# Causal mask of the key-major scores: a VectorE addition in place of a TensorE product

## What is computed

```
q = (x @ Wq) as 32 heads;  k, v = halves of x @ Wkv       # one key/value head
scores = q k^T / sqrt(32) + slope[h] * (kpos - qpos)
scores = where(kpos <= qpos, scores, -inf)                # the causal mask
attn = softmax(scores) @ v;  x = layernorm(x + attn @ Wo)
x = layernorm(x + x @ W^T + b + lora_of_selected_rank(x))
```

## Time and profile before

| what | value |
|---|---|
| median of three runs | 3512.88 us (3511.38 to 3514.06) |
| the profiled execution | 3511.45 us, span of its records 3509.7 us |
| attention proper (first to last S) | 55.6 to 2647.7 us of the span |
| mean granted TensorE clock | 0.978 of full speed |

### The profile page before, as it was taken

One profiled execution on the slowest core, in us unless ns is written; L12 is line 12 of the kernel. 1 busy time (PEld: TensorE's weight loads), 2 busy tenths in 40 slices (PEclk: granted clock), 3 DMA queues, 4 the chain that ended last, 5 costly groups with the idle time before them and its releaser, 6 DMA issues. The chain is left out here.

```text
span 3509.7 us, 55953 instructions
## 1 busy us (share of the span) xinstructions
PE 3387.2 (97%) x20577; PEld 2208.8 (63%) x20577; DVE 2120.3 (60%) x5166; ACT 1715.1 (49%) x3076; POOL 1593.7 (45%) x484
## 2 busy tenths in 40 slices
PE   6989999999999999999999999999997999999998
PEld 4655555555655554555555555555535999999997
DVE  4556667776877662566676677876723545454544
ACT  2536647667656666546566666666673101010100
POOL 1114536666577775125356656676892101010100
PEclk8999999999999999999999999999997999999999
DMA  3531221111110112332131211111102121212121
GB/s 103 146 91 56 73 71 52 49 49 53 42 52 25 49 32 81 111 88 79 52 88 43 58 28 52 43 28 40 58 31 85 55 72 54 72 54 72 54 72 43
DMA packets 214076, 215.45 MB, mean 61 GB/s; under 512 B 13876, under 2 KB 162356, under 8 KB 213784
## 3 DMA queue, kind: packets, MB, share of 16 engines
q1 hardware_dynamic: 213848, 212.46, 20.6%
HBM read 144.72 MB, written 67.17 MB: 60 GB/s over the span
## 5 line engine op out<-in xcount | busy, mean ns | idle before, releaser
L1041 ACT ACTIVATE prob<-ps_s,alibi 128x512 f32<-128x512 f32 (+3 forms) x2049 | 1220.1, 630 | 698.8 <-PE ps_s L1314 658.7
L976 POOL TENSOR_TENSOR prob<-prob 128x2048 f32<-128x2048 f32 (+1 forms) x240 | 1043.7, 4367 | 314.8 <-PE ps_o L1321 235.7
L1158 DVE TENSOR_REDUCE mxp<-ps_a 128x1 f32<-128x512 f32 x1536 | 972.8, 682 | 345.2 <-PE ps_a L1297 339.0
L1297 PE MATMUL ps_a<-wol,qst 97*128 97x512 f32 (+3 forms) x2560 | 934.9, 383 | 36.3 <-DVE mxp L1158 11.4
L1314 PE MATMUL ps_s<-qst,kexp 97*128 97x512 f32 (+3 forms) x2049 | 832.9, 411 | 5.5 <-ACT prob L1041 4.7
L1161 DVE CUSTOM_DVE_ANT_0 ps_a<-ps_a,maska 128x128 f32<-128x128 f32 (+3 forms) x1024 | 484.9, 513 | 305.4 <-PE ps_a L1297 282.6
L1263 PE MATMUL ps_m<-woh,wol 128*128 128x512 f32 x1704 | 646.6, 412 | 4.5 <-POOL wol L961 4.4
L1297 PEld LDWEIGHTS ps_a<-wol,qst 97*128 97x128 f32 x2560 | 486.7, 192 | 200.3 <-DVE mxp L1158 68.8
L1321 PE MATMUL ps_o<-prob,val 128*32 128x512 f32 (+3 forms) x5120 | 565.1, 537 | 11.4 <-ACT prob L1041 8.7
L1314 PEld LDWEIGHTS ps_s<-qst,kexp 97*128 97x128 f32 x2049 | 400.6, 196 | 193.4 <-ACT prob L1041 117.7
L961 POOL TENSOR_TENSOR wol<-wq_raw,wol 128x1024 fp32r<-128x1024 f32 x64 | 152.4, 2381 | 653.1 <-ACT wol L1016 653.1
(11 more groups left out here) (133 smaller groups left out, 3415.9 us busy)
## 6 DMA issues: line engine op xcount, KB each, us to landing
qst<-q_rows SPq DMA_DIRECT2D x192, 256.0 KB, 3.9
work<-in_L_attn_hidden_states SPq DMA_DIRECT2D x64, 512.0 KB, 4.9
wq_raw<-in_L_attn_Wq SPq DMA_DIRECT2D x64, 512.0 KB, 4.8
q_rows<-wol SPq DMA_DIRECT2D x128, 256.0 KB, 2.0
att_scratch<-at_sb SPq DMA_DIRECT2D x64, 256.0 KB, 2.5
at_raw<-att_scratch SPq DMA_DIRECT2D x32, 512.0 KB, 5.3
out<-work SPq DMA_DIRECT2D x32, 512.0 KB, 3.1
work<-in_L_attn_Wo SPq DMA_DIRECT2D x8, 512.0 KB, 4.4
```

What stands on the lines that cost most here:

```text
L976: nc.gpsimd.tensor_tensor(even[:, :, c1:], even[:, :, c1:], odd[:, :, c1:], ALU.add).then_inc(pair_done, 1)
L1041: nc.scalar.activation(prob[slot_of(step)][:, h, c0:], bank[:, c0:], ACT.Exp, bias=alibi_of(g, h, k - full_tiles(g))).then_inc(e_done, 1)
L1158: nc.vector.tensor_reduce(top, ps, AX.X, ALU.max).then_inc(a_done, 1)
L1297: last = nc.tensor.matmul(bank[:, 0:cols], qst[g % 3][0:KR, h, t * P:(t + 1) * P], kmax[0:KR, ring(sg):ring(sg) + cols], start=True, stop= ...
```

## The change

The mask products and `identb` go. `maskt` becomes f32, and VectorE adds it to the 128 diagonal columns of the score bank in place, between the score matmul and the exponential. The exponential of a diagonal tile waits for a new counter, `masked`, where it waited for `s_full`. The planner books 270 ns on VectorE (its next item 190 ns after) in place of 41 ns on TensorE, and so writes a different order.

```diff
+def masks_until(g, k, h):
+    return GH * (QT * g + k - full_tiles(g)) + h + 1
...
         if k >= full_tiles(g):
-            self.pe, end = self.pe + 41, end + 41
+            end = self.on_dve(end + 37, 270, 190) - 4
...
-        identb = sb(ctx, "identb", [P, P], BF16)
-        maskt = sb(ctx, "maskt", [P, P], BF16)
+        maskt = sb(ctx, "maskt", [P, P], F32)
...
-                act.wait_ge(s_full, START + scored + 1)
+                if k >= full_tiles(g):
+                    act.wait_ge(masked, START + masks_until(g, k, h))
+                else:
+                    act.wait_ge(s_full, START + scored + 1)
...
+            def mask(g, k, h, bank, scored):
+                c0 = (k - full_tiles(g)) * P
+                tile = bank[:, c0:c0 + P]
+                dve.wait_ge(s_full, START + scored + 1)
+                nc.vector.tensor_tensor(tile, tile, maskt[:], ALU.add).then_inc(masked, 1)
...
                 if what == "A":
                     maximum(n, *arg, banks[bank], at)
+                if what == "S" and arg[0] >= full_tiles(n):
+                    mask(n, *arg, banks[bank], at)
...
-                if diagonal:
-                    nc.tensor.matmul(bank[:, c0:c0 + P], identb[:], maskt[:], start=True, stop=False,
-                                     skip_group_check=True)
                 last = nc.tensor.matmul(bank[:, c0:], kexp[0:KR, at:at + P], qst[g % 3][0:KR, h, c0:],
-                                        start=not diagonal, stop=True, skip_group_check=True)
+                                        start=True, stop=True)
```

More of the change, by code:

```diff
@@ L815, in attention @@
         s_full = counter("s_full")
+        masked = counter("masked")
         e_done = counter("e_done")
@@ L939, in _ @@
             nc.gpsimd.memset(ident[:], 0.0).then_inc(pool_c, 1)
-            nc.gpsimd.memset(identb[:], 0.0).then_inc(pool_c, 1)
             nc.gpsimd.memset(maska[:], 0.0).then_inc(pool_c, 1)
@@ L944, in _ @@
             nc.gpsimd.iota(dist_i[:], [[P, DIST0 + QT]], base=-P * DIST0, channel_multiplier=1).then_inc(pool_c, 1)
+            pool.wait_ge(pool_c, 5)
+            nc.gpsimd.iota(kpos_i[3 * DH:KR], [[1, QB]], base=0, channel_multiplier=0).then_inc(pool_c, 1)
             pool.wait_ge(pool_c, 6)
[L946 to L950, removed]
+            nc.gpsimd.affine_select(out=ident[:], in_=ident[:], compare_op=ALU.not_equal, fill=1.0, base=0,
+                                    pattern=[[-1, P]], channel_multiplier=1).then_inc(pool_c, 1)
             nc.gpsimd.affine_select(out=maska[:, QB - P:], in_=maska[:, QB - P:], compare_op=ALU.is_ge, fill=MASKED, base=0,
@@ L954, in _ @@
                                     pattern=[[1, P]], channel_multiplier=-1).then_inc(pool_c, 1)
-            pool.wait_ge(pool_c, 11)
+            pool.wait_ge(pool_c, 9)
             nc.gpsimd.memset(kexp[3 * DH:KR].bitcast(F32), 1.0).then_inc(ones_row, 1)
@@ L1102, in distances @@
             def distances():
-                dve.wait_ge(pool_c, 7)
+                dve.wait_ge(pool_c, 6)
                 nc.vector.tensor_copy(dist[:], dist_i[:]).then_inc(dist_done, 1)
@@ L1227, in _ @@
         def _(pe):
-            pe.wait_ge(pool_c, 11)
+            pe.wait_ge(pool_c, 9)
             pe.wait_ge(slope_set, NH)
@@ L1308, in scores @@
                 c0 = max(0, k - full_tiles(g)) * P
-                diagonal = k >= full_tiles(g)
                 at = key_tile(g, k) * P
-                if diagonal:
-                    nc.tensor.matmul(bank[:, c0:c0 + P], identb[:], maskt[:], start=True, stop=False,
-                                     skip_group_check=True)
                 last = nc.tensor.matmul(bank[:, c0:], kexp[0:KR, at:at + P], qst[g % 3][0:KR, h, c0:],
-                                        start=not diagonal, stop=True, skip_group_check=True)
+                                        start=True, stop=True)
                 last.then_inc(s_full, 1)
```

## The result

The changed kernel took 3585.84 us as the median of four runs (3569.97 to 3591.40), the kernel before 3512.26 (3511.38 to 3514.06): a ratio of 1.0201, 95% interval 1.0166 to 1.0237. It is 74 us slower, where 43 us faster was forecast, and lies outside the range.

The account below looks back on a forecast made before the run. TensorE was taken to set the pace over most of the attention. Terms -123 + 20 + 30 + 19 + 11 = -43 us took the profiled 3511.45, plus 1.4 for the median, to 3470 us; range 3398 to 3530.

Parts of the forecast that it names:

- What the change removes: TensorE, diagonal tiles: dropping 1,024 mask products at 0.12 us each saves 123 us, if TensorE sets the pace at each.
- What it adds: VectorE: 1,024 additions of 128x128 at 0.24 us each in the queue (ends 0.127 and 0.315), 246 us in all.
- What waits behind it: Runs of diagonal tiles: TensorE waits for VectorE from the fourth tile on, costing 20 + 30 + 19 us.
- What moves: Planner's new order: 53 more returns from P or U to wide products at 0.21 us each, 11 us.
- Rival 2: Diagonal tiles: VectorE becomes the bound, every pair with an A at 0.85 us; 3639, in part slower by less; chance 0.18.
- Rival 1: Attention: no new waits, since the planner's P, U and Q cover VectorE everywhere; 3401 us; chance 0.19.
- Rival 3: Attention stages: another engine ends them, so waits fill the product's removal; 3513 us, give or take 10; chance 0.13.

## Why the prediction was wrong

Its sum was -123 for the products, 69 for waits in runs, and 11 for what moves. Measured along the same path (product out, then the order, then the additions) it is -58, +85 and +48, or +75 (with the order first: +74, -47 and +48). The miss of 118 us is 65 from the first term and 74 from the last, with 21 back from the one between.

- **"What the change removes" failed.** The price of 0.12 us was right where TensorE sets the pace: pairs without a mask came at 0.46. The condition, "if TensorE sets the pace at each of them", was not. The text itself had 0.61 us of VectorE beside 0.593 of TensorE and read it as "nobody waited"; it should have read that a pair with an A can get no shorter than 0.61 for long, and asked the same of ScalarE, whose exponentials of 512 columns follow one another at 0.58. 65 of the 123 us did not appear. Unit 25 shows both limits in their place; VectorE's, taken away everywhere, gave back 13 us, and what ScalarE's covers on the whole was not measured.
- **"What it adds" held**, with 0.20 in the queue in place of 0.24 and a record of 300 ns, inside the bounds of 0.127 and 0.315.
- **"What waits behind it" came near, 48 against 69, partly by luck.** The mechanism, pairs at VectorE's pace from the fourth or fifth tile on, shows in both orders. But the lag was counted from pairs at 0.463, which without any mask do not last either (0.57 and 0.60 at unit 25), so part of this term stands in the first one already. And P and U cover the rest only in an order made for it: in the order of before the same additions cost 182 us.
- **"What moves" failed by its size**, 85 in place of 11. I counted returns from P to wide products and nothing else. In the new order A's wait for VectorE and U for GpSimd's sums more often; halving the maxima did not shorten the distance of 85, halving exponentials and sums as well brought it to 35 in the kernels with neither mask, and halving the sums alone took the distance of the change to the kernel before from 74 to 64. Only part of the 85 is traced; the rest stays open.
- **Rival 2's mechanism, "in part", is shown**: VectorE at 0.80 a pair paces the diagonal. But in the order of the change that is worth 48 us, about what the product's removal gave there (47); the loss itself is the order's. The rival's full price, 3639, lies near the 3634.9 of the additions in the order of before; as it counted pairs of the other order, that is not a proof. Rival 1 is refuted. Rival 3's mechanism, waits that fill what the product leaves, holds for half of the removal.
- The Trainium skill, page "Perfetto Trace Analysis", section "Identifying the Most-Contended Engine", judges TensorE's headroom by the busy share of its weight loads (or by its arithmetic against the peak, not worked out here); by those loads VectorE, not TensorE, was the more contended engine. On the diagonal the runs bear that out in part: with additions VectorE's 0.80 us set the distance of the pairs, but without a mask ScalarE's 0.58 stood as close as VectorE's 0.61.

## What to carry to other kernels

Before a removed instruction is credited with its time, write down the next limit of every engine at that very place: here VectorE's and ScalarE's stood 0.02 us from the pair's 0.593, and half of the gain was never there. Where a planner sets the order from prices, an edit is two edits; run the old order with the new work, and the new order with the old work, before explaining anything. When two engines are near balance, moving a third of the work can win where moving all of it loses.

## What was not expected of the hardware

A product whose bank was released late cost TensorE more than its wait. The weight loads of the changed kernel at unit 25 (idle before in brackets):

```profile
1012.41 0.19 PEld L1310 LDWEIGHTS ps_a<-wol,qst 97*128 97x128 f32 x1 [0.50 <-DVE mxp L1163]
1012.54 0.19 PEld L1323 LDWEIGHTS ps_m<-qst,kexp 97*128 97x128 f32 x1
1013.21 0.19 PEld L1310 LDWEIGHTS ps_a<-wol,qst 97*128 97x128 f32 x1 [0.48 <-DVE mxp L1163]
```

The A released at 1012.41 has load and product begin together, and the next S's load follows at 1012.54. The A's record is 0.50 us in place of 0.39, and the next product starts 0.34 after it (1012.75) in place of 0.23 (1010.90 to 1011.13). The same 0.34 follows the A at 1013.21. So these two late releases each cost 0.11 us behind the release, beside the wait: the A at 1012.41 comes 0.45 after its S (1011.96) in place of 0.23. That a weight load which no product covers is the reason is how the rows look, no run tests it; and the 0.50 in brackets is idle time of the loads, during part of which TensorE still worked on the S ahead.
